# Two engines change the order of two operations inside each step of the second half of the attention

## The chip, the cores and the metric

The kernel runs on one core of a Trainium2 chip. The metric is the time of one execution on the device, in microseconds; below 0.2% (about 4 us here) a change can't be told from none. Five engines matter: PE (TensorE, matrix products), DVE (VectorE), ACT (ScalarE), POOL (GpSimd) and SP, which only issues DMAs. Each engine works off its own list of instructions in order, and they wait for one another on semaphores.

## The reference, cut to what matters

One decoder layer on x of 16 sequences, 128 tokens, 512 columns, in float32:

```
x = x + attention(layernorm(x))          # 16 heads of 128, rms-normed q and k, rope, tanh softcap, causal
x = x + wkv(w, u, layernorm(x), ctx)     # a recurrence over the 128 tokens, channel by channel
x = x + experts(layernorm(x))            # 16 experts, 6 of them per token, and a shared one

# attention, per head:
scores = 50 * tanh(q @ k.T * scale / 50); masked above the diagonal; attn = softmax(scores)
out = attn @ v;  result += out @ wo.T
# wkv, per token t:
no  = max(o, u + k_t);   y = (exp(o - no) p + exp(u + k_t - no) v_t) / (exp(o - no) q + exp(u + k_t - no))
no2 = max(w + o, k_t);   p, q, o = (exp(w + o - no2) p + exp(k_t - no2) v_t,  the same with q and 1,  no2)
```

## The kernel before, in words

Every float32 product is made of three faster ones: each operand is split into a high part (the rounded copy, written by ACT) and a low part (the operand minus its high part, written by DVE or POOL), and PE multiplies high by high, high by low and low by high.

The attention runs in 128 steps and three more that drain it. A step is one pair of heads of one sequence. Its work is spread over four steps by software: in step s PE makes q and k (L976) and v (L1001) of item s (`front`), the scores (L1037) of item s-1 (`mid`), the product of probabilities and v (L1013) and the transposes of its result (L1049) of item s-2 (`back`), and the output product (L1027) of item s-3 (`tail`). PE's order in one step is L976, the transposes of q and k (L166), L1001, L1013, L1027, L1037, L1049. The score part of a step goes: PE scores, ACT tanh (L1245) and exp (L1249) into `ex`, POOL multiplies `ex` by the causal mask (L1422), ACT copies it to the high part of `pT` (L1256), DVE subtracts to get its low part (L1649). L1013 of the next step waits for both parts. DVE then begins the next step with the sums of squares (L1598), the low part of q and k (L1601), which L1037 waits for, and the normalized output (L1616), which L1049 waits for. ACT's part of that is the squares (L1217), for which L1598 waits, and the high part (L1220).

The recurrence needs attention results of finished sequences only. The first half (64 steps) takes the first eight sequences through all eight pairs of heads; the second half takes four sequences at a time. In the second half `rec` is true: one item of the recurrence's own list is worked off in each step (`rec_pe`, `rec_act`, `rec_dve`, `rec_pool`, `rec_pool_norm`, `rec_sp`). A pair of sequences takes a cycle of 11 steps (PITCH), numbered r = 0 to 10 in what follows; two pairs overlap, one in its front part and the one before in its back part. The 64 steps hold the cycles 0 to 4 and nine steps of cycle 5. What the list holds, by r:

| r | DVE (`rec_dve`) | POOL (`rec_pool`, then `rec_pool_norm`) | ACT, at the end of the step |
|---|---|---|---|
| 0 | L482 low part of a row tile; L486 qS*e | L443 pS+vS | L363; L393, which waits for L486 |
| 1 | L490 pS*qS, waits for L447 | L447 pS*e | L373 |
| 2 | L508 scan; L511 | - | - |
| 3 | L498 | L452 | - |
| 4 | L498 | L455 | L401 twice |
| 5 | L494 scan; layer norm statistics (L141 to L148) | L458 | - |
| 6 | - | L462; L152 and L155 | L411, L413 |
| 7 | L518 scan | - | L411, L413 |
| 8 | L518 scan; L523 | - | L419 |
| 9 | L482; L527 | L466 | L423, which waits for L527 |
| 10 | layer norm statistics | L471; L152 and L155, which wait for the statistics | L390 |

Within a step the order on each engine is written out by hand. On DVE the recurrence's item stands after the output's low part (L1637) and ahead of L1649. On POOL it stands after the small operations of the step (L1408, L1411) and the split of a weight piece (L177, which the second half has only in its last four steps) and ahead of the mask (L1422). After the attention come the shared expert's steps (`shared_step`), in which the rest of the recurrence runs, and the routed experts.

Of the kernel before, what the change touches and what calls it, by code (L numbers as in the profile page):

```python
# [56 lines left out]
def build(nc, x, ctxT, weights, qw, kw, cos, sin, wkv_w, wkv_u, gateT, out):  # L57
# [7 lines left out]
    with ExitStack() as ctx:  # L65
# [197 lines left out]
        SPLIT = NSTEP_B // 2  # L263
# [172 lines left out]
        def rec_pool(pool, w):  # L436

            p, r = w // PITCH, w % PITCH
            q, k = p, p - 1
            if r == 0 and 0 <= k < NQ:  # L440
                pool.wait_ge(ev_done, k + 1)
                pool.wait_ge(pm_done, k + 1)
                pool.tensor_tensor(pS[:, :, 0:T], pS[:, :, 0:T], vS[:, :, :], ALU.add).then_inc(num_done, 1)  # L443
            if r == 1 and 0 <= k < NQ:
                pool.wait_ge(num_done, k + 1)
                pool.wait_ge(inv_done, k + 1)
                pool.tensor_tensor(pS[:, :, 0:T], pS[:, :, 0:T], e2[:, :, 1:T + 1], ALU.mult).then_inc(first_done, 1)  # L447
            if not 0 <= p < NQ:
                return
            if r == 3:  # L450
                pool.wait_ge(o_scan, q + 1)
                pool.tensor_tensor(a2[:, :, 1:T + 1], oS[:, :, 0:T], oS[:, :, 1:T + 1],  # L452
                                   ALU.subtract).then_inc(d2_done, 1)
            if r == 4:
                pool.tensor_tensor(e2[:, :, 1:T + 1], kS[:, :, 1:T + 1], oS[:, :, 1:T + 1],  # L455
                                   ALU.subtract).then_inc(e2a_done, 1)
            if r == 5:
                pool.tensor_tensor(dE[:, :, :], kS[:, :, 1:T + 1], oS[:, :, 0:T], ALU.subtract).then_inc(d_done, 1)  # L458
            if r == 6:
                pool.wait_ge(e2_done, q + 1)  # L460
                pool.wait_ge(v_in, 16 * q + 16)
                pool.tensor_tensor(e2v[:, :, 1:T + 1], e2[:, :, 1:T + 1], vS[:, :, :], ALU.mult).then_inc(e2v_done, 1)  # L462
            if r == 9:
                pool.wait_ge(pscan, 2 * q + 2)
                pool.wait_ge(aA_done, q + 1)
                pool.tensor_tensor(pS[:, :, 0:T], pS[:, :, 0:T], aA[:, :, :], ALU.mult).then_inc(pm_done, 1)  # L466
            if r == 10:
                pool.wait_ge(dE_done, q + 1)
                pool.wait_ge(e2v_done, q + 1)
                pool.wait_ge(den_done, q + 1)  # L470
                pool.tensor_tensor(vS[:, :, :], dE[:, :, :], vS[:, :, :], ALU.mult).then_inc(ev_done, 1)  # L471
# [312 lines left out]
        with nc.Block() as block:  # L784
# [588 lines left out]
            def _(pool):  # L1373
# [29 lines left out]
                def step(s, at4, fw, b, g):  # L1403
                    par = at4 % 2
                    front, mid, back, tail, rec = wants(s)
                    if front:
                        pool.wait_ge(ms_done, s + 1)
                        pool.tensor_tensor(rr[:, :], rr[:, :], expo[:, :], ALU.pow).then_inc(pw_done, 1)  # L1408
                        wait(pool, th_done, 2 * s - 2)
                        pool.wait_ge(pw_done, s + 1)  # L1410
                        pool.tensor_tensor(rk[:, par, :], rr[:, HG:4], kscale[:, :], ALU.mult).then_inc(rms_done, 1)  # L1411

                        for n in pieces_of(s):
                            if isinstance(n, int):
                                piece_pool(pool, n, n % 2, (n // HB) % 2, bass.ds(n % HB * PIECE, PIECE))
                            else:
                                piece_pool(pool, n, par, 1 - fw, bass.ds(b * PIECE, PIECE))
                    if rec:
                        rec_pool(pool, s - SPLIT)
                    if mid:  # L1420
                        pool.wait_ge(ex_done, s)
                        pool.tensor_tensor(heads(ex), heads(ex), mask[:, :, :], ALU.mult).then_inc(mask_done, 1)  # L1422
                    if row_tile(s + 1) is not None and s % 2 == 1:
                        ln_pool(pool, row_tile(s + 1) // 2, 0)
                    if rec:
                        rec_pool_norm(pool, s - SPLIT)
                attention(pool, step)
# [90 lines left out]
            def _(dve):  # L1518
# [74 lines left out]
                def step(s, at4, fw, b, g):  # L1593
                    par = at4 % 2
                    front, mid, back, tail, rec = wants(s)
                    if front:
                        dve.wait_ge(sq_done, s + 1)
                        dve.reduce_sum(ssq[:, :], sq.rearrange("p (g n) -> p g n", g=4), AX.X).then_inc(ss_done, 1)  # L1598
                    if mid:
                        dve.wait_ge(qkT_hi, s)  # L1600
                        dve.tensor_tensor(qkT[:, 1, :], QT_[:, :], qkT[:, 0, :].bitcast(F32),  # L1601
                                          ALU.subtract).then_inc(qkT_lo, 1)
                    if front:
                        wait(dve, rms_done, s)
                        dve.wait_ge(ss_done, s + 1)
                        dve.tensor_scalar(rr[:, :], ssq[:, :], 1.0 / DH, RMS_EPS, ALU.mult, ALU.add)\  # L1606
                            .then_inc(ms_done, 1)
                        dve.wait_ge(v_hi, s + 1)
                        dve.tensor_tensor(vE[:, at4, 1, :, 0:DH], heads(V_[:, 0:256]),
                                          vE[:, at4, 0, :, 0:DH].bitcast(F32), ALU.subtract).then_inc(v_lo, 1)  # L1610
                    if back:
                        dve.wait_ge(pv_done, s - 1)
                        av = O_[:, 0:HG * 130].rearrange("p (h n) -> p h n", h=HG)
                        dve.reciprocal(rden[:, :], av[:, :, DH]).then_inc(rden_done, 1)
                        dve.wait_ge(rden_done, s - 1)
                        dve.tensor_tensor(heads(on), av[:, :, 0:DH],  # L1616
                                          rden[:, :].unsqueeze(2).to_broadcast([P, HG, DH]),
                                          ALU.mult).then_inc(on_done, 1)
                    if front:
                        dve.wait_ge(pw_done, s + 1)  # L1620
                        dve.wait_ge(k_out, s + 1)
                        if isinstance(s, int) and s == HB:
                            dve.wait_ge(tabs, 14)
                        for h in range(HG):
                            dve.scalar_tensor_tensor(out=rot[:, h * DH:(h + 1) * DH],
                                                     in0=bank[par][:, h * DH:(h + 1) * DH], scalar=rr[:, h:h + 1],
                                                     in1=rope[:, bass.ds(g * (2 * P) + h * DH, DH)], op0=ALU.mult,
                                                     op1=ALU.mult).then_inc(rot_done, 1)
                    if row_tile(s - 1) is not None:
                        row_lo(row_tile(s - 1), stage[:, row_tile(s - 1) % 2], R_)  # L1630
                    if tail:
                        dve.wait_ge(wo_done, s - 2)
                        bb = behind(s, fw, b, 3)[1]
                        dve.tensor_tensor(xres[:, bb, :], xres[:, bb, :], Y_[:, :], ALU.add).then_inc(acc_done, 1)
                    if back:
                        dve.wait_ge(oT_hi, s - 1)
                        dve.tensor_tensor(oT[:, 1, :, :], heads(OT_[:, 0:256]), oT[:, 0, :, :].bitcast(F32),  # L1637
                                          ALU.subtract).then_inc(oT_lo, 1)
                    if row_tile(s + 1) is not None and s % 2 == 1:
                        n = row_tile(s + 1)  # L1640
                        dve.wait_ge(ld_x, 16 if n < 10 else 32)
                        ln_stats(dve, n // 2, n, 0, used=n)
                    if isinstance(s, int) and 1 <= s <= 12:
                        constants(s)
                    if rec:
                        rec_dve(dve, s - SPLIT)
                    if mid:
                        dve.wait_ge(p_hi, s)
                        dve.tensor_tensor(pT[:, 1, :, :], heads(ex), pT[:, 0, :, :].bitcast(F32),  # L1649
                                          ALU.subtract).then_inc(p_lo, 1)  # L1650

                attention(dve, step)

# [135 lines left out]
```

## Time and profile before

| | |
|---|---|
| time, median of 3 runs | 2057.85 us (2057.79 to 2061.95) |
| the profiled execution, its own time | 2063.05 us |
| its span | 2061.3 us |
| PE busy | 1993.2 us, 97% |
| DVE, ACT, POOL busy | 1073.2, 922.6, 1013.0 us |
| second half of the attention | about 519 to 1045 us of the span |

Busy time is the sum of an engine's instructions. A row of the timeline reads: start, duration, engine, line of the kernel, operation, what it writes <- what it reads, count of instructions merged; in brackets the idle time of the engine just before it and who ended it.

### The profile page before, as it was taken

The numbers are of one execution on the slowest core, as the hardware profiler recorded it, in microseconds if no ns is written. First come the engines' busy times: TensorE is split into PE (matmuls) and PEld (weight loads), VectorE is DVE, ScalarE is ACT, GpSimd is POOL, SyncE is SP. The second block draws the span as 40 slices with busy tenths as digits, with TensorE's granted clock in tenths as the row PEclk, the third lists the DMA queues.
The fourth block names the chain that finished last, engine by engine and source line by source line (L and its number), as shares of the span: only waits on it lengthen the run. The fifth ranks groups of instructions, "written<-read, shape, count | busy, mean of one in ns | idle before, by whom it ended". The sixth has DMA issues, their size and how long they took to land.

```text
span 2061.3 us, 40646 instructions
## 1 busy us (share of the span) xinstructions
PE 1993.2 (97%) x12136; PEld 1804.6 (88%) x12137; DVE 1073.2 (52%) x2351; ACT 922.6 (45%) x2119; POOL 1013.0 (49%) x1076
## 2 busy tenths in 40 slices
PE   6999999999999999999878999899999999999998
PEld 5888888888888888888768899799999999999997
DVE  4765555555667766777666655333333333333332
ACT  4655555554565666657555412233333333233232
POOL 5444444442344444444556206666733333488885
PEclk9999999999999999999989999999999999999999
DMA  9677777777877868777635237666643343499899
GB/s 319 222 235 247 257 249 251 246 245 274 299 257 270 324 238 316 269 264 280 215 95 186 93 102 264 226 205 212 230 137 121 121 127 125 133 214 222 192 215 244
DMA packets 188986, 450.48 MB, mean 219 GB/s; under 512 B 21696, under 2 KB 21952, under 8 KB 188864
## 3 DMA queue, kind: packets, MB, share of 16 engines
q1 hardware_dynamic: 135392, 338.68, 47.8%
q0 software_dynamic: 21504, 51.13, 10.5%
q10 hardware_dynamic: 31968, 59.12, 8.9%
q8 instruction: 67, 1.10, 0.2%
q14 instruction: 55, 0.45, 0.1%
HBM read 275.36 MB, written 173.48 MB: 218 GB/s over the span
## 4 chain that ended last, share of the span: by engine, by line
PE 89%; DMA 3%; POOL 2%; DVE 2%; issue 2%; ACT 1%; SPq 1%; ACTq 0%; POOLq 0%
PE bank L1125 21%; PE bank L976 16%; PE bank L1135 11%; PE bank L1027 8%; PE bank L1001 8%; PE bank L166 6%; PE bank L579 5%; PE bank L1013 4%; PE bank L1037 4%; PE bank L589 3%; PE bank L596 2%; PE bank L1049 1%; DMA xT<-xT_att 1%; DMA raw<-in_weights 1%; POOL w_lo L177 1%
## 5 line engine op out<-in xcount | busy, mean ns | idle before, releaser
L1125 PE MATMUL bank<-w_hi,xT 128*128 x1776 | 473.8, 329 | 2.1 <-DVE xT L1713 2.1
L976 PE MATMUL bank<-w_hi,xT 128*128 128x512 f32 x1024 | 354.3, 407 | 5.0 <-DMA xT<-xT_att 3.5
L1408 POOL TENSOR_TENSOR rr<-rr,expo 128x4 f32<-128x4 f32 x128 | 128.9, 1007 | 423.7 <-DVE rr L1606 423.7
L606 DVE TENSOR_TENSOR hT<-bank,hT 128x384 fp32r<-128x384 f32 x143 | 79.7, 558 | 475.1 <-ACT hT L603 475.1
L1125 PEld LDWEIGHTS bank<-w_hi,xT 128*128 128x128 f32 x1776 | 315.9, 188 | 9.4 <-issue 4.0
L1125 PE MATMUL bank<-w_lo,xT 128*128 x888 | 286.4, 323 | 0.0
L976 PEld LDWEIGHTS bank<-w_hi,xT 128*128 128x128 f32 x1024 | 195.4, 191 | 45.8 <-issue 5.3
L1135 PE MATMUL bank<-w_hi,hT 128*128 x666 | 229.9, 399 | 2.7 <-DVE hT L606 2.5
L603 ACT ACTIVATE hT<-bank 128x384 fp32r<-128x384 f32 x143 | 70.2, 491 | 329.6 <-PE bank L596 315.7
L1001 PE MATMUL bank<-w_hi,xT 128*128 128x256 f32 x1024 | 214.7, 293 | 0.0
L976 PE MATMUL bank<-w_lo,xT 128*128 128x512 f32 x512 | 202.1, 395 | 0.0
L1027 PE MATMUL bank<-w_hi,oT 128*128 128x512 f32 x512 | 189.7, 411 | 0.0
L1245 ACT ACTIVATE th<-bank,rk 128x128 f32<-128x128 f32 x256 | 80.1, 364 | 229.4 <-PE bank L1037 229.4
L1125 PEld LDWEIGHTS bank<-w_lo,xT 128*128 128x128 f32 x888 | 168.1, 189 | 4.2
L1001 PEld LDWEIGHTS bank<-w_hi,xT 128*128 128x128 f32 x1024 | 167.1, 189 | 0.0
L1492 POOL DMA_INDIRECT xres<-yg,a x96 | 148.9, 1551 | 30.3 <-issue 27.4
L1422 POOL TENSOR_TENSOR ex<-ex,mask 128x256 f32<-128x256 f32 x128 | 97.7, 763 | 123.5 <-ACT ex L1249 123.5
L1135 PEld LDWEIGHTS bank<-w_hi,hT 128*128 128x128 f32 x666 | 124.9, 188 | 32.4 <-issue 5.6
L1001 PE MATMUL bank<-w_lo,xT 128*128 128x256 f32 x512 | 144.4, 282 | 0.0
L1598 DVE TENSOR_REDUCE ssq<-sq 128x4 f32<-128x512 f32 x128 | 87.7, 685 | 108.3 <-ACT sq L1217 108.2
L1464 POOL DMA_INDIRECT xg<-xnB,a x96 | 93.8, 977 | 92.0 <-DVE a L708 60.6
L579 PE MATMUL bank<-w_hi,xT 128*128 128x352 f32 x512 | 136.9, 329 | 0.0
(242 smaller groups left out, 4432.6 us busy)
## 6 DMA issues: line engine op xcount, KB each, us to landing
xT<-xT_att SPq DMA_DIRECT2D x126, 512.0 KB, 5.2
w_hi<-w_split SPq DMA_DIRECT2D x64, 512.0 KB, 6.7
w_lo<-w_split SPq DMA_DIRECT2D x64, 512.0 KB, 7.7
xg<-blank SPq DMA_DIRECT2D x111, 264.0 KB, 4.7
yg<-blank SPq DMA_DIRECT2D x111, 256.0 KB, 5.9
raw<-in_weights SPq DMA_DIRECT2D x82, 272.0 KB, 3.1
w_split<-w_hi SPq DMA_DIRECT2D x64, 272.0 KB, 3.4
w_split<-w_lo SPq DMA_DIRECT2D x64, 272.0 KB, 3.7
```

The source lines that it names most:

```text
L166: last = pe.transpose(out[:, c * P:(c + 1) * P], src(c), ident[:, :])
L579: last = pe.matmul(out[:, 0:I], xT[:, par, a, c * P:(c + 1) * P], w_hl[w][:, fw, at:at + I], start=n == 0, stop=n == 11)
L976: last = pe.matmul(bank[par][:, :], xT[:, par, a, c * P:(c + 1) * P], w_hl[w][:, fw, c * 512:(c + 1) * 512], start=n == 0, stop=n == 11)
L1001: last = pe.matmul(V_[:, 0:256], xT[:, par, a, c * P:(c + 1) * P], w_hl[w][:, fw, at:at + 256], start=n == 0, stop=n == 11)
L1027: last = pe.matmul(Y_[:, :], oT[:, a, h, :], w_hl[w][:, bw, at:at + D], start=n == 0, stop=n == 5)
L1125: last = pe.matmul(out_[:, 0:I], xT[:, par, a, c * P:(c + 1) * P], flat(w_hl[w])[:, bass.ds(at + (c * 2 * I + half_ * I), I)], start=n == ...
L1135: last = pe.matmul(out_[:, :], hT[:, a, c * P:(c + 1) * P], flat(w_hl[w])[:, bass.ds(at + (W2_AT + c * D), D)], start=n == 0, stop=n == 3 ...
L1408: pool.tensor_tensor(rr[:, :], rr[:, :], expo[:, :], ALU.pow).then_inc(pw_done, 1)
L1422: pool.tensor_tensor(heads(ex), heads(ex), mask[:, :, :], ALU.mult).then_inc(mask_done, 1)
L1464: pool.indirect_dma_start(out=xg[:, :], out_offset=bass.IndirectOffsetOnAxis(ap=slot_i[:, k, b:b + 1], axis=0), in_=xnB[:, b, :], in_offse ...
L1492: pool.indirect_dma_start(out=xres[:, b, :], out_offset=None, in_=yg[:, :], in_offset=bass.IndirectOffsetOnAxis(ap=slot_i[:, k, b:b + 1], ...
L1598: dve.reduce_sum(ssq[:, :], sq.rearrange("p (g n) -> p g n", g=4), AX.X).then_inc(ss_done, 1)
```

## The change

In the steps of the attention (`step` of POOL and of DVE) two blocks swap places. POOL applies the mask (L1422) ahead of `rec_pool`; `rec_pool_norm` stays last. DVE makes the low part of the probabilities (L1649) ahead of `rec_dve`. No instruction is added or removed, and no wait changes. In the first half, where `rec` is false, the order is the same as before.

```diff
@@ POOL, step @@
-                    if rec:
-                        rec_pool(pool, s - SPLIT)
                     if mid:
                         pool.wait_ge(ex_done, s)
                         pool.tensor_tensor(heads(ex), heads(ex), mask[:, :, :], ALU.mult).then_inc(mask_done, 1)
                     if row_tile(s + 1) is not None and s % 2 == 1:
                         ln_pool(pool, row_tile(s + 1) // 2, 0)
+                    if rec:
+                        rec_pool(pool, s - SPLIT)
                     if rec:
                         rec_pool_norm(pool, s - SPLIT)
@@ DVE, step @@
-                    if rec:
-                        rec_dve(dve, s - SPLIT)
                     if mid:
                         dve.wait_ge(p_hi, s)
                         dve.tensor_tensor(pT[:, 1, :, :], heads(ex), pT[:, 0, :, :].bitcast(F32),
                                           ALU.subtract).then_inc(p_lo, 1)
+                    if rec:
+                        rec_dve(dve, s - SPLIT)
```

## Rows read from the trace of the kernel before

**Rows 1.** The page, busy time by engine:
```profile
PE 1993.2 (97%) x12136; PEld 1804.6 (88%) x12137; DVE 1073.2 (52%) x2351; ACT 922.6 (45%) x2119; POOL 1013.0 (49%) x1076
```

**Rows 2.** Waits of PE, 585 to 1060 us: total us, times, longest:
```profile
PE bank L1013 <- issue: 10.7, 6, 3.3
```

**Rows 3.** Timeline, 827 to 838 us, a step with r = 5 and the next:
```profile
827.51 2.40 POOL L458 TENSOR_TENSOR dE<-kS,oS 128x1024 f32<-128x1024 f32 x1
...
829.32 0.42 ACT L1249 ACTIVATE ex<-th 128x256 f32<-128x256 f32 x1
...
829.87 0.74 POOL L1422 TENSOR_TENSOR ex<-ex,mask 128x256 f32<-128x256 f32 x1
...
830.38 2.38 DVE L494 TENSOR_TENSOR_SCAN qS<-a,e 128x1032 f32<-128x1032 f32 x1
...
834.35 0.42 DVE L1649 TENSOR_TENSOR pT<-ex,pT 128x256 fp32r<-128x256 f32 x1
834.68 0.68 DVE L1598 TENSOR_REDUCE ssq<-sq 128x4 f32<-128x512 f32 x1
834.87 0.86 PE L1013 MATMUL bank<-vE,pT 128*128 128x130 f32 x6 [1.37 <-issue]
...
837.63 0.41 PE L1049 MATMUL bank<-ident,on 128*128 128x128 f32 x2
```

**Rows 4.** DVE against POOL: timeline at 1068 and 519 us; lines (duration ns min/median/max):
```profile
1068.73 2.21 POOL L443 TENSOR_TENSOR pS<-pS,vS 128x1024 f32<-128x1024 f32 x1
...
1068.87 3.14 DVE L486 TENSOR_TENSOR qS<-qS,e 128x1024 f32<-128x1024 f32 x1
...
518.90 0.42 DVE L1649 TENSOR_TENSOR pT<-ex,pT 128x256 fp32r<-128x256 f32 x1
...
519.07 0.80 POOL L152 TENSOR_TENSOR rstd<-rstd,expo 128x2 f32<-128x2 f32 x1 [1.67 <-DVE rstd L148]
...
L486 DVE TENSOR_TENSOR qS<-qS,e x8: 1215/1440/3143, 609.6 to 1158.0; 128x1024 f32<-128x1024 f32 x8
...
L152 POOL TENSOR_TENSOR rstd<-rstd,expo x24: 692/722/1469, 6.4 to 1179.3; 128x2 f32<-128x2 f32 x24
```

**Rows 5.** Timeline, 860 to 869 us, a step with r = 9 and the next:
```profile
860.42 2.19 POOL L466 TENSOR_TENSOR pS<-pS,aA 128x1024 f32<-128x1024 f32 x1
...
861.55 0.42 ACT L1249 ACTIVATE ex<-th 128x256 f32<-128x256 f32 x1
...
862.61 0.68 DVE L482 TENSOR_TENSOR stage<-bank,stage 128x512 fp32r<-128x512 f32 x1
863.21 1.22 DVE L527 TENSOR_TENSOR qS<-qS,dE 128x1024 f32<-128x1024 f32 x1
...
866.65 0.69 DVE L1598 TENSOR_REDUCE ssq<-sq 128x4 f32<-128x512 f32 x1 [1.89 <-ACT sq L1217]
...
868.93 0.44 PE L1049 MATMUL bank<-ident,on 128*128 128x128 f32 x2
```

**Rows 6.** Timeline, 869 to 874 us, the step with r = 10:
```profile
869.39 2.41 POOL L471 TENSOR_TENSOR vS<-dE,vS 128x1024 f32<-128x1024 f32 x1
...
870.58 0.42 ACT L1249 ACTIVATE ex<-th 128x256 f32<-128x256 f32 x1
...
873.53 0.42 DVE L1649 TENSOR_TENSOR pT<-ex,pT 128x256 fp32r<-128x256 f32 x1
...
873.96 0.69 DVE L1598 TENSOR_REDUCE ssq<-sq 128x4 f32<-128x512 f32 x1
```

**Rows 7.** Timeline, 877 to 883 us, the step with r = 0:
```profile
877.67 0.42 ACT L1249 ACTIVATE ex<-th 128x256 f32<-128x256 f32 x1
...
879.33 1.34 DVE L486 TENSOR_TENSOR qS<-qS,e 128x1024 f32<-128x1024 f32 x1
...
882.28 0.69 DVE L1598 TENSOR_REDUCE ssq<-sq 128x4 f32<-128x512 f32 x1 [1.28 <-ACT sq L1217]
```

**Rows 8.** Busy us of each engine (xcount), PEclk granted, DMA share, GB/s, 1018 to 1025 us:
```profile
1018.00:1025.00 7.00, 6.41 (x22) 5.71 (x23) 3.88 (x12) 3.97 (x11) 5.03 (x5) 0.51 0.21 52
```

## The prediction

> **What bounds the kernel now.** I read the page first: PE is busy 97% of the span [rows 1], so almost every microsecond that PE stands still is a microsecond of the kernel, and time can be won or lost only there. The view of waits for PE, cut to the second half of the attention, then shows what there is to win: 10.7 us in six waits of L1013, the longest 3.3 [rows 2]. The releaser is not named ("issue"), but the timeline names it [rows 3]: in a step with r = 5, DVE goes from the scan L494 at 830.38 through the layer norm statistics to L1649 at 834.35, and L1013, which needs its result, starts at 834.87 after an idle of 1.37. So 3.97 us of recurrence stand ahead of a 0.42 us operation that PE needs. The other thing to see there is who paces PE when DVE is late: L1049 needs L1616, a fixed distance behind L1598. In rows 5, L1049 starts 2.28 after L1598 (866.65 to 868.93), and that is the shortest distance there can be; in rows 3 it is 2.95 (834.68 to 837.63), so there L1049 had 0.67 us in hand. The question for each step is therefore when L1598 starts.
>
> **The change, part by part.** POOL's mask now starts as soon as the exp is done: 0.05 after it, and it takes 0.74 (L1422 in rows 3). In rows 3 it started 0.13 after the exp's end (829.74 to 829.87) because L458 ended only then, so this gain is 0.1 us; elsewhere up to 0.8 us. The probabilities' low part no longer waits for the recurrence, so the six waits of rows 2 should go. That is the plus side, and for PE it is worth nothing by itself if the same recurrence work then delays L1598.
>
> What is late next is just that. Two things are added ahead of L1598. First, L1649 must wait for mask and copy before DVE's recurrence may begin, where DVE used that time. Second, and larger, POOL's recurrence operation used to run beside DVE operations that read PSUM; now it starts when the mask ends, about 0.5 us before L1649 is ready to start (the 0.42 us copy lies between), and lies across L1649 and what follows it. Rows 4 show what happens when two such operations meet: L486, which reads two SBUF tensors and takes 1.22 at its shortest, started 0.14 after POOL's L443 and took 3.14. L443 ended at 1070.94 and L486 at 1072.01, 1.07 later: it stood still until L443 was through, with 0.15 of its start-up hidden. L1649 is of the same kind (`ex` and `pT` are both in SBUF), and in the other direction it is seen to hold POOL up: POOL's L152, 0.69 at its shortest, took 0.80 beside it and ended 0.55 after L1649's end (519.32 to 519.87). No row shows L1649 itself behind a long POOL operation. Its cost there is between 0 and the whole POOL operation less the 0.5 us head start, 1.4 to 1.9 us; I take the upper end, since L486 is the nearest row: L1649 ends 0.27 (0.42 less 0.15) after POOL's recurrence operation.
>
> The Trainium skill, page "SBUF — State Buffer", section "Who interferes with whom", says that a VectorE instruction with two SBUF inputs contends with a GpSimd instruction that reads SBUF and that the one issued first blocks the other fully; by it the upper end holds for L1649 too. The page "Advanced Engine Details and Errata", section "Mode Summary", names only VectorE's two-port modes as interfering, and a float32 tensor_tensor is not one; by that alone neither L1649 nor L486 would wait, and the sum would be the third rival's below. The 3.14 us of L486 [rows 4] speaks for the first.
>
> Now each costly step, as exp's end + 0.05 + mask 0.74 - 0.04 (POOL operations overlap by that) + POOL's operation + 0.27 = L1649's end, then DVE's recurrence (each starting 0.07 before the last ends), then L1598:
> - r = 5 [rows 3]: exp ends 829.74, L458 takes 2.40, L1649 ends 833.16. The scan and the statistics take 3.97, so L1598 starts at 837.06 instead of 834.68. L1049 follows at +2.28, 839.34 instead of 837.63: **+1.7 us**. The wait of L1013 is gone, and a longer one of L1037 and L1049 stands in its place. Without any blocking L1649 would end at 831.4, L1598 start at 835.3 and L1049 at 837.6: nothing won or lost.
> - r = 9 [rows 5]: exp ends 861.97, L466 takes 2.19, L1649 ends 865.18. L482 takes 0.60 to L527, and L527 1.22: it ends at 866.93. L423 on ACT waits for L527, and ACT's squares come after it. One such ACT operation and the squares put 1.61 between DVE's end and L1598 (L486 ends 880.67, L1598 starts 882.28, rows 7). So L1598 starts at 868.54 instead of 866.65: **+1.9**, and L1049 with it.
> - r = 10 [rows 6]: exp ends 871.00, L471 takes 2.41, L1649 ends 874.43. The statistics are 3.97 less the scan's 2.31, 1.66: L1598 at 876.02 instead of 873.96, **+2.1**.
> - r = 0 [rows 7]: exp ends 878.09, L443 takes 2.21 [rows 4], L1649 ends 881.32. L482 and L486 (0.60 + 1.22) end at 883.07, and L1598 starts 1.61 later, 884.68 instead of 882.28, +2.4. PE is ahead of DVE in this stretch, so the exp can come up to 0.9 us earlier against the L1598 before it (estimate); I take **+1.6**.
> - The other steps: r = 1 and 3 to 8 have 0.7 to 2.4 us of recurrence on DVE, and by the same sum L1598 starts up to 1.4 us late in them. L1049's slack in a step is about as much (estimate; 0.67 was left even in rows 3, in which PE had waited 1.37): nothing, at most 0.3 each.
>
> r = 9, 10 and 0 follow one another with PE waiting for DVE, so their delays add: 5.6 us. The second half holds five such groups, the first with little in it (no L482, no back part): 4 x 5.6 + 3 = 25.4 us. It holds six steps with r = 5: four like rows 3, 4 x 1.7 = 6.8; the first, without statistics and without a wait before, +1.7; the last, which has the 3.3 us wait of rows 2 in it and weight pieces on POOL, +0.5 (it may as well gain 2). Sum: 34.4 us.
>
> **The clock.** After the 3.3 us wait the granted clock was 0.51 over the next 7 us [rows 8], half of 2.4 GHz; at half speed that cost about 3.4 us. After the waits of 1.37 it stayed full. The new waits with r = 5 are about 3 us long, close to the one that lost the clock, and PE must work at full pace behind them. Between 0 and 4 x 3.4 = 14 us: I take 5.
>
> Against the profiled execution, 2063.05 us, the sum gives 2063.05 + 34.4 + 5 = 2102.5. That execution was 5.2 us above the median of 2057.85, so for the median I forecast 2097 us.
>
> **The rivals.**
> - L1649 isn't blocked, only the long DVE operations are (L527, L486). Then r = 5 costs nothing, r = 9 about 1 us and r = 0 about 0.6, 8 to 10 us in all: 2067 us. For it: no row shows L1649 blocked. Against: it reads two SBUF tensors as L486 does, and holds up L152.
> - Faster: L1013's waits go and L1049's slack takes up the rest. That is 4 x 1.6 and the 3.3 us wait with its clock loss, 3.3 + 3.4: 13 us, 2045 us. It decides by whether L1598 of the step after r = 5 starts by about 833.7 (L1049 would fall due at 837.63 - 1.6 = 836.0, less 2.28). Against: the scan and statistics alone end at 834.7 even if they start right behind a free L1649 at 830.8.
> - No blocking of any kind, as the second page has it: only the time DVE loses before its recurrence counts, 0.5 to 0.6 us for r = 9, 10 and 0 in each group, 5 x 1.5 = 7 us: 2065 us.
> - The clock falls after nearly every wait of 2 us and more: 14 us and more instead of 5, 2110 to 2120 us.
>
> **How the numbers follow.** Forecast 70%, its own range 2084 to 2110; first and third rival together 14%; faster 7%; the clock 9%. I give 2066 to 2114, which holds the forecast, the two mild cases' upper part and half of the last. Under 0.2% (4 us) a difference can't be told: faster 0.07, same 0.03, slower 0.90.
>
> **What the changed profile would show.** L1649 with a median near 2 us in steps with POOL work, against 0.42 now: the central step, and if it stays at 0.42 the first rival holds. No waits of L1013 in the second half, and in their place waits of L1049 for L1616 and of L1037 for L1601. L1598 later than now by the four numbers above, counted from the step's exp. A PEclk below 9 between 600 and 1000 us for the clock term. Wrong would be a second half no longer than now, or L1013 still waiting.

## The result, and the profile after

The change makes the kernel slower. Measured together: 2103.99 us (median of 4 runs, 2098.17 to 2107.05) against 2058.82 us before (2057.79 to 2061.95), a ratio of 1.021, 95% interval 1.0194 to 1.0225 (the ratios in this document are estimated over all runs of a series and differ a little from the quotient of the two medians). The forecast was 2097 in a range of 2066 to 2114, with 0.90 for slower. The profiled execution took 2107.05 us (forecast for it: 2102.5), its span 2105.3.

The page after, busy time by engine (answers to [rows 1]), the same page's row of the probabilities' low part (now L1647; the mask is now L1420), and its PEclk row, in tenths:

```profile
PE 2013.5 (96%) x12136; PEld 1815.2 (86%) x12137; DVE 1135.6 (54%) x2351; ACT 926.0 (44%) x2119; POOL 1012.8 (48%) x1076
...
PEclk8999999999999999999998999999999999999999
...
L1647 DVE TENSOR_TENSOR pT<-ex,pT 128x256 fp32r<-128x256 f32 x128 | 122.2, 955 | 71.2 <-ACT pT L1256 71.1
```

The same instructions on every engine; DVE is busy 62.4 us longer. The 64 low parts of the second half took 26.6 us together before and 95.1 after, 68.5 more: that is more than all of it, and some of DVE's other operations got shorter (the scan L494: median 2.41 before, 2.29 after).

The waits of PE in the second half (total us, times, longest), answering to [rows 2]:

```profile
PE bank L1037 <- ACT qkT L1220: 17.8, 10, 2.0
PE bank L1037 <- issue: 15.7, 9, 2.8
PE bank L1013 <- issue: 3.4, 5, 1.4
PE bank L976 <- DMA xT<-xT_att: 0.9, 2, 0.7
PE bank L1013 <- ACT pT L1256: 0.8, 1, 0.8
```

The waits of L1013 fell from 10.7 to 3.4 us, and 33.5 us of L1037 stand where 0.9 us stood before. That is the whole trade in five lines: PE waits little for the probabilities now; it waits for the next item's q and k instead.

The timeline after, the step with r = 5 that answers to [rows 3]:

```profile
854.97 0.42 ACT L1249 ACTIVATE ex<-th 128x256 f32<-128x256 f32 x1
855.46 0.74 POOL L1420 TENSOR_TENSOR ex<-ex,mask 128x256 f32<-128x256 f32 x1 [0.92 <-ACT ex L1249]
856.16 2.42 POOL L458 TENSOR_TENSOR dE<-kS,oS 128x1024 f32<-128x1024 f32 x1
856.24 0.42 ACT L1256 ACTIVATE pT<-ex 128x256 fp32r<-128x256 f32 x1 [0.58 <-POOL ex L1420]
856.69 2.17 DVE L1647 TENSOR_TENSOR pT<-ex,pT 128x256 fp32r<-128x256 f32 x1 [0.57 <-ACT pT L1256]
858.78 2.29 DVE L494 TENSOR_TENSOR_SCAN qS<-a,e 128x1032 f32<-128x1032 f32 x1
...
858.98 0.83 PE L1013 MATMUL bank<-vE,pT 128*128 128x130 f32 x6
...
862.65 0.68 DVE L1598 TENSOR_REDUCE ssq<-sq 128x4 f32<-128x512 f32 x1
...
864.03 1.51 PE L1037 MATMUL bank<-qkT 128*128 128x128 f32 x6 [2.76 <-issue]
```

L458 runs from 856.16 to 858.58. L1647 starts 0.53 behind it and ends at 858.86, 0.28 after it, though alone it takes 0.42. L1598 starts 7.26 after the exp's end. L1037 then takes 1.51 instead of 0.86: the granted clock has fallen to half of 2.4 GHz, as the window behind it shows (PEclk is the third number from the end; answers to [rows 8]):

```profile
863.30:870.10 6.80, 6.07 (x19) 5.14 (x20) 5.11 (x11) 2.64 (x7) 4.58 (x5) 0.50 0.90 364
```

The same in the steps with r = 9 and 10 (answering to [rows 5] and [rows 6]):

```profile
892.66 2.20 POOL L466 TENSOR_TENSOR pS<-pS,aA 128x1024 f32<-128x1024 f32 x1
...
893.19 1.96 DVE L1647 TENSOR_TENSOR pT<-ex,pT 128x256 fp32r<-128x256 f32 x1 [0.58 <-ACT pT L1256]
...
898.49 0.69 DVE L1598 TENSOR_REDUCE ssq<-sq 128x4 f32<-128x512 f32 x1 [1.61 <-ACT sq L1217]
...
903.60 2.39 POOL L471 TENSOR_TENSOR vS<-dE,vS 128x1024 f32<-128x1024 f32 x1
...
904.12 2.14 DVE L1647 TENSOR_TENSOR pT<-ex,pT 128x256 fp32r<-128x256 f32 x1 [0.57 <-ACT pT L1256]
...
907.86 0.68 DVE L1598 TENSOR_REDUCE ssq<-sq 128x4 f32<-128x512 f32 x1
```

**Where the 44 us went, step by step.** PE paces the attention, so the gap between the L1049 of successive steps is the length of a step; the gap at r runs from the L1049 of that step to that of the next. The table has the gap after minus the gap before, taken from the two timelines, for each r and each of the cycles 0 to 5. The rows left out hold 0.1 or less, except one 0.94 at r = 2 (a wait of L976 for its DMA) and -2.4 at r = 8 of cycle 5, the last gap, which lies behind the stretch measured next (there the kernel before has a wait of L1013 of 1.95 us and a fall of the clock).

```
r     cycle 0     1     2     3     4     5     sum
9          1.33  1.92  1.42  1.92  1.92         8.5
10         1.69  1.73  1.83  1.49  1.71         8.4
0          0     0.76  1.99  2.34  2.23  1.99   9.3
1          0     0.05  0.84  1.61  1.89  1.52   5.9
4          0.07  0.07  0.05  0.05  0.06 -2.21  -1.9
5          1.56  1.94  1.66  2.07  1.98 -1.02   8.2
6          0.02  1.06  0.02  2.21  1.03  0.98   5.3
```

With the 0.94 at r = 2, and without the last gap, it is 44.6 us; the second half, from L1598 of its first step to that of its last, went from 516.6 to 560.7 us. What follows it took 1023.9 us after and 1025.4 before. So the loss lies in the steps that the prediction named, and in the steps with r = 1 and 6 right behind them, to which it gave no wait.

The -2.21 at r = 4 of cycle 5 is a wait for a DMA in the profiled execution of the kernel before; nothing in the runs ties it to the change.

```profile
1002.90 0.47 PE L976 MATMUL bank<-w_hi,xT 128*128 128x512 f32 x1 [2.02 <-DMA xT<-xT_att]
```

Waits of L976 of this kind come at other places in other executions (1.43 us at about 997 in the second run of the one-mask kernel below, 1.76 at about 650 in the second run with filler), so differences of about 2 us between the second halves of two profiles can be chance. The changed kernel's second half was 560.7 us in this profile and 557.7 in another.

Below, "second half" is that span. It is also what is compared between chips: on one of them (the runs against 2126.35 us below) the kernel before was some 65 us slower. In the kernels profiled there the extra lies behind the second half (1085.1 us in the one-mask kernel, against 1025.7 on the other chip). Times are compared only with the kernel before on the same chip.

### The profile page after: what moved, and what is told of

Its sections match the earlier page's. It is cut to its first block, busy times and chain, and to the rows that moved or that the text cites. A ratio compares the mean times of both kernels' runs of the same rounds, so it can differ in the third digit from the quotient of the medians.

```text
span 2105.3 us, 40646 instructions
## 1 busy us (share of the span) xinstructions
PE 2013.5 (96%) x12136; PEld 1815.2 (86%) x12137; DVE 1135.6 (54%) x2351; ACT 926.0 (44%) x2119; POOL 1012.8 (48%) x1076
## 4 chain that ended last, share of the span: by engine, by line
PE 82%; DVE 5%; issue 4%; POOL 3%; DMA 3%; ACT 2%; SPq 1%; ACTq 0%; POOLq 0%
PE bank L1125 20%; PE bank L976 14%; PE bank L1135 11%; PE bank L1027 7%; PE bank L1001 7%; PE bank L166 5%; PE bank L579 4%; PE bank L1037 3%; PE bank L1013 3%; PE bank L589 3%; PE bank L596 2%; DMA xT<-xT_att 1%; PE bank L1049 1%; DVE pT L1647 1%; POOL rr L1408 1%
## 5 line engine op out<-in xcount | busy, mean ns | idle before, releaser
L976 PE MATMUL bank<-w_hi,xT 128*128 128x512 f32 x1024 | 365.6, 419 | 3.5 <-DMA xT<-xT_att 2.4
L1125 PEld LDWEIGHTS bank<-w_hi,xT 128*128 128x128 f32 x1776 | 315.8, 188 | 9.3 <-issue 3.9
L976 PEld LDWEIGHTS bank<-w_hi,xT 128*128 128x128 f32 x1024 | 202.7, 198 | 47.0 <-DMA xT<-xT_att 2.8
L976 PE MATMUL bank<-w_lo,xT 128*128 128x512 f32 x512 | 208.1, 406 | 0.0
L1420 POOL TENSOR_TENSOR ex<-ex,mask 128x256 f32<-128x256 f32 x128 | 94.8, 740 | 171.7 <-ACT ex L1249 171.7
L1001 PEld LDWEIGHTS bank<-w_hi,xT 128*128 128x128 f32 x1024 | 167.4, 190 | 0.1
L1647 DVE TENSOR_TENSOR pT<-ex,pT 128x256 fp32r<-128x256 f32 x128 | 122.2, 955 | 71.2 <-ACT pT L1256 71.1
L1037 PEld LDWEIGHTS bank<-qkT 128*128 128x128 f32 x768 | 105.0, 193 | 52.9 <-ACT qkT L1220 21.9
```

What stands on the lines that cost most here:

```text
L976: last = pe.matmul(bank[par][:, :], xT[:, par, a, c * P:(c + 1) * P], w_hl[w][:, fw, c * 512:(c + 1) * 512], start=n == 0, stop=n == 11)
L1001: last = pe.matmul(V_[:, 0:256], xT[:, par, a, c * P:(c + 1) * P], w_hl[w][:, fw, at:at + 256], start=n == 0, stop=n == 11)
L1037: last = pe.matmul(S_[:, h * T:(h + 1) * T], qkT[:, a, (HG + h) * T:(HG + h + 1) * T], qkT[:, w, h * T:(h + 1) * T], start=n == 0, stop=n ...
L1125: last = pe.matmul(out_[:, 0:I], xT[:, par, a, c * P:(c + 1) * P], flat(w_hl[w])[:, bass.ds(at + (c * 2 * I + half_ * I), I)], start=n == ...
```

## The experiments

**DVE's half alone.** DVE in the new order, POOL in the old one.

```diff
@@ DVE, step; POOL as before @@
-                    if rec:
-                        rec_dve(dve, s - SPLIT)
                     if mid:
                         dve.wait_ge(p_hi, s)
...
+                    if rec:
+                        rec_dve(dve, s - SPLIT)
```

> DVE's half of the change alone: the low part of the probabilities ahead of the recurrence on DVE, POOL's order as before. Theory A (a DVE operation with two SBUF inputs and a POOL operation exclude each other; in the changed kernel POOL's recurrence operation lies on L1649 and the DVE recurrence): here POOL's operation is over before the mask, so the low-part operation keeps its 0.42 us, but it has to wait for mask and copy, which POOL's operation delays by up to 0.8 us, and DVE's recurrence waits behind it. From the timeline of before: r = 5 about 0, r = 9 +0.9, r = 10 +1.1, r = 0 +1.6 us, in 4.5 groups 16 us, so 2070 to 2078 us; few or no falls of the clock before 1000 us. Rival B (no blocking; what costs in the changed kernel is that POOL's results arrive 2 to 3 us later and the recurrence's chain becomes late): POOL's order is untouched, so at most +7 us, 2058 to 2065 us.

Measured: 2082.9 us against 2060.31, ratio 1.0102 (1.0085 to 1.0119), above the 2070 to 2078 expected. The low part takes 0.42 to 0.43 us in each step, and still half of the loss is there. The waits of PE and the step with r = 5:

```profile
PE bank L1037 <- ACT qkT L1220: 15.6, 10, 1.9
PE bank L1037 <- issue: 9.3, 11, 2.8
...
839.91 2.40 POOL L458 TENSOR_TENSOR dE<-kS,oS 128x1024 f32<-128x1024 f32 x1
...
843.48 0.43 DVE L1647 TENSOR_TENSOR pT<-ex,pT 128x256 fp32r<-128x256 f32 x1 [0.61 <-ACT pT L1256]
843.82 2.30 DVE L494 TENSOR_TENSOR_SCAN qS<-a,e 128x1032 f32<-128x1032 f32 x1
```

So moving DVE's recurrence behind the low part has a price of its own. By the table's measure it is 1.0 to 1.6 (r = 9), 0.5 to 0.8 (10), 1.9 to 2.3 (0, from the third cycle on), and nothing at r = 5 but in the last cycle. The expectation had 0.9 for r = 9, and few or no falls of the clock before 1000 us: there are three, behind the waits of r = 0, at 1.6 us each.

**POOL's half alone.** POOL in the new order, DVE in the old one (the diff's POOL part).

> POOL's half alone: the mask ahead of POOL's recurrence operation, DVE's order as before. Theory A: POOL's operation now lies on DVE's own recurrence operations. L527 and L486 should take 2 to 3 us instead of 1.2 to 1.5, L494 either its 2.4 (if it gets hold first) or 4.5, the low part 0.42 in most steps and up to 1 us with r = 10. Sum per cycle 2.9 to 4.6 us, 13 to 21 us in all: 2070 to 2080 us. Rival B: POOL's results are as late as in the changed kernel, so most of its +45 us should be here, over 2085 us, while the durations of DVE's operations stay as before.

Measured: 2089.33 us, 1.0127 (1.0109 to 1.0145). The time is in the range that was to speak against the theory (over 2085 us), but the durations of DVE's operations, which were to stay as before in that case, show blocking, and the cost is more than the expectation had counted:

```profile
846.18 2.34 DVE L494 TENSOR_TENSOR_SCAN qS<-a,e 128x1032 f32<-128x1032 f32 x1
846.31 4.36 POOL L458 TENSOR_TENSOR dE<-kS,oS 128x1024 f32<-128x1024 f32 x1
...
850.68 0.41 DVE L1649 TENSOR_TENSOR pT<-ex,pT 128x256 fp32r<-128x256 f32 x1
...
851.20 1.29 PE L1013 MATMUL bank<-vE,pT 128*128 128x130 f32 x6 [1.91 <-issue]
...
858.11 1.96 DVE L1649 TENSOR_TENSOR pT<-ex,pT 128x256 fp32r<-128x256 f32 x1 [0.57 <-ACT pT L1256]
```

Here DVE's scan began 0.13 before POOL's L458 and kept its 2.34; L458 took 4.36 instead of 2.40 and ended 2.15 after the scan. So each engine can hold up the other: in these rows and in those of the changed kernel the operation that started first kept its time, and the other stood until it was over. That is called the lock in what follows. With DVE in the old order L1649 is blocked too where DVE has nothing or little to do before it (1.96 in the row at 858.11, r = 6). L1013 waits 21.7 us in all, twice the figure before. Neither half of the change gains.

**Whose cost is the blocked low part?** The changed kernel, with POOL holding its recurrence back until the low part is made.

```diff
+                        pool.wait_ge(p_lo, s)
                         rec_pool(pool, s - SPLIT)
```

> The changed kernel with one wait more: POOL begins its recurrence operation only when the low part of the step's probabilities is done. POOL's results arrive later still, but L1649 (L1647 in it) has no POOL operation beside it. Theory A: its duration falls from a median of about 2 us in steps with POOL work to 0.42; r = 5 gets back 1.7 us and r = 10 about 1.3 (r = 9 and r = 0 nothing, since L527 and L486 are then blocked in its place), 15 us in all, and some of the falls of the clock go: 2080 to 2090 us, that is faster than the changed kernel's 2104 although a wait was added. Rival B: every result of POOL is later, so it is slower than the changed kernel, over 2106 us.

Measured: 2098.16 us, 1.0173 (1.0155 to 1.0191), between the two theories' ranges. The low part fell to 0.42 in every step, as foretold. In the first five steps with r = 5 and in those with r = 10 together, 10.4 us came back. At r = 9 and 0 nothing did from the second group on, because POOL's operation now meets what is next on DVE:

```profile
901.59 0.42 DVE L1648 TENSOR_TENSOR pT<-ex,pT 128x256 fp32r<-128x256 f32 x1 [0.56 <-ACT pT L1256]
...
902.09 2.39 POOL L471 TENSOR_TENSOR vS<-dE,vS 128x1024 f32<-128x1024 f32 x1 [0.99 <-DVE pT L1648]
...
903.13 0.30 DVE L144 BATCH_NORM_AGGREGATE mv<-st 128x2 f32<-128x6 f32 x2
...
903.46 1.05 DVE L147 TENSOR_SCALAR nmean<-mv 128x2 f32<-128x2 f32 x1
904.43 0.15 DVE L148 TENSOR_SCALAR rstd<-mv 128x2 f32<-128x2 f32 x1
...
910.26 2.20 POOL L443 TENSOR_TENSOR pS<-pS,vS 128x1024 f32<-128x1024 f32 x1 [0.99 <-DVE pT L1648]
...
910.70 2.85 DVE L486 TENSOR_TENSOR qS<-qS,e 128x1024 f32<-128x1024 f32 x1
```

L486 took 2.85 instead of 1.21 and ended 1.09 after L443. And L147, an operation on two columns that takes 0.17 alone, stood until L471 was through (904.48), while the statistics ahead of it (L141, L144) passed freely. By the table: r = 5 costs 0.5 instead of 1.6 and r = 10 0.8 to 1.0 instead of 1.7, but r = 9 and 0 cost 1.5 to 2.3 and 2.1 to 2.5. That the collision moves there instead of ending, the expectation had said. What it had not is that r = 1 and 6 lose 9 us more than in the changed kernel: the clock falls eleven times, and 6.3 us are one step (r = 1, cycle 1) in which L976 waited 3.21 us for its DMA, with a fall of 6.8 us behind it. Why that load came late is not shown.

**Is the lock held for a whole instruction?** The changed kernel, each of POOL's eight recurrence operations cut in two halves of 128x512.

```diff
+            for h in (slice(0, KC), slice(KC, 2 * KC)):
+                pool.tensor_tensor(out[:, h, :], a[:, h, :], b[:, h, :], op).then_inc(done, 1)
```

(and the waits for these semaphores count twice as far)

> The changed kernel with each of POOL's eight recurrence operations (128x1024) in two halves (128x512), every result the same. Theory A, that L1649 (L1647 here) stands still until the POOL instruction that began before it is over: the first half takes about 1.2 us (0.74 for 256 elements and 2.2 for 1024 give 0.26 + 0.48 per 256), L1647 is ready 0.5 after its start and ends 0.27 after its end, so its duration in steps with POOL work falls from 1.96 to 2.16 us to about 1.0. The second half then lies on DVE's recurrence instead, so the time changes little, 2095 to 2105 us. Rival: the two engines share bandwidth while they overlap; then L1647 overlaps POOL's work as long as before and its duration stays at about 2 us.

Measured: 2161.73 us against 2126.35, 1.018 (1.0125 to 1.0236); second half 550.8 us, 9.9 and 6.9 below the changed kernel's two profiles. The step with r = 5:

```profile
852.88 2.73 POOL L438 TENSOR_TENSOR dE<-kS,oS 128x512 f32<-128x512 f32 x2
853.41 1.04 DVE L1649 TENSOR_TENSOR pT<-ex,pT 128x256 fp32r<-128x256 f32 x1 [0.57 <-ACT pT L1258]
854.37 3.40 DVE L496 TENSOR_TENSOR_SCAN qS<-a,e 128x1032 f32<-128x1032 f32 x1
```

The low part fell from 2.17 to 1.04: it got through between the halves. Then the second half met the scan, which took 3.40 instead of 2.29. So the lock is held for one instruction at a time; two engines that share bandwidth for as long as they overlap would have left the low part as it was.

**What must leave the step with r = 5?** The kernel before, with the variance and mean of the row tile (the statistics, 1.66 us of DVE) taken one step later, from r = 5 to r = 6, in which DVE has nothing else. Order of both engines as before.

```diff
-            if r == 5 and back:
+            if r == 6 and back:
```

> The kernel before with one edit: the layer norm statistics of the recurrence (1.66 us on DVE) move from r = 5 to r = 6, where DVE has nothing. By the timeline of before, L1649 of r = 5 then ends 8.3 us after L1598 and L1013 falls due at 8.6: the four waits of 1.4 us (1.6 us in the spacing of the matmuls) go, and the last, of 3.3 us, shrinks by 0.5 only, because there the mask is held up by L494. L1598 of the next step comes 1.7 earlier too, so nothing takes their place. 4 x 1.6 + 0.5 = 7 us: 2050 to 2053 us. The rival: the statistics delay ACT's norm in r = 7 or L1598 after r = 6 by as much, 2057 to 2060 us.

Measured: 2052.67 us against 2060.31, 0.9966 (0.9949 to 0.9983); on another chip, in the run below, 0.9955. Faster than both kernels. In that second run the second half takes 507.4 us, 9.2 less than before. The table's measure is -1.6 in each of four steps with r = 5. In the last cycle it is -2.6 at r = 5, with 1.5 lost again at r = 6, and -2.1 at r = 4, which is the DMA wait of 2.02 us that the kernel before had there; so some 7 us are the edit's. What the change wanted, L1013 not waiting for the probabilities, comes in these four steps from less work in the full step, not from another order.

**The same in the changed kernel.**

> The changed kernel with the layer norm statistics moved from r = 5 to r = 6 on DVE, as in the run e5. By the sum of the prediction L1598 after r = 5 comes 1.66 us earlier, so the waits of L1037 there shrink by as much, 5 x 1.7 = 8 us, and the falls of the clock behind them (four or five of the ten in the second half) go, up to 6 us more: 2088 to 2098 us. It stays 35 us or more above the same edit without the change (2052.7), since r = 9, 10 and 0 are as in the changed kernel. Rival: with the list of DVE at r = 5 short, putting the low part first costs nothing any more, and it comes to within 10 us of 2052.7.

Measured: 2154.26 against 2126.35, 1.0116 (1.0062 to 1.0171); second half 546.0, 14.7 and 11.7 us below the changed kernel's two profiles and 38.6 above the last one. Steps with r = 5 and 6 together cost 0.6 instead of 1.6; r = 9, 10 and 0 cost the same 1.9, 1.7 and 2.0 to 2.3. The three steps are independent of the statistics, as the sum had them.

**The mask early in one step alone.** The kernel with later statistics, in which L1013 still waited 2.7 us behind the last step with r = 5; POOL's mask ahead of its recurrence there and nowhere else.

```diff
-                    if rec:
+                    if rec and s != NSTEP_B - 4:
                         rec_pool(pool, s - SPLIT)
                     if mid:
...
+                    if rec and s == NSTEP_B - 4:
+                        rec_pool(pool, s - SPLIT)
```

> The run e5 (statistics at r = 6, otherwise the kernel before) with POOL's half of the change in one step only, the first of the last four steps (r = 5 of the last cycle), where POOL also splits two weight pieces and the mask began at 7.7 and took 2.7 us because L494 had got ahead of it. With the mask before POOL's recurrence operation it starts at 5.4, L494 gets ahead of POOL's operation instead (as the run e2 showed, where L494 took 2.34 and L458 4.37), and L1649 ends at 8.7 us against 8.6 at which L1013 falls due. The wait of 2.9 us there and the fall of the clock behind it (3.4 us) go: 5 us less than e5, 2046 to 2050 us. Rival: POOL's operation, which then ends at about 10.7, delays L1408 of the next step and through it the transposes of L166, and the gain is gone: 2052 us.

Measured: 2113.79 us against 2126.35, 0.9948 (0.9922 to 0.9974); second half 506.5 us, 0.8 below that of the kernel with later statistics alone (507.3 in its first run), not 5. The step, from the second run of it; the last row is the same L1013 without the early mask, from the second run of that kernel:

```profile
1006.30 2.64 DVE L494 TENSOR_TENSOR_SCAN qS<-a,e 128x1032 f32<-128x1032 f32 x1
1006.73 4.36 POOL L458 TENSOR_TENSOR dE<-kS,oS 128x1024 f32<-128x1024 f32 x1
...
1008.86 2.52 DVE L1651 TENSOR_TENSOR pT<-ex,pT 128x256 fp32r<-128x256 f32 x1
...
1011.48 0.86 PE L1013 MATMUL bank<-vE,pT 128*128 128x130 f32 x6 [2.06 <-issue]
...
1011.59 0.86 PE L1013 MATMUL bank<-vE,pT 128*128 128x130 f32 x6 [2.69 <-ACT pT L1256]
```

A chain of locks: the scan holds up L458, and L458, once it has the lock, holds up the low part until it ends at 1011.09. L1013 waits 2.06 instead of 2.69. Even the one early mask takes only 0.6 us off a wait of 2.7, since the long operation put behind it holds up the low part in turn.

**The clock.** The changed kernel, with products that nothing reads ahead of the waits for the low part of q and k, 282 of them in the steps with r = 6, 10 and 1, some 36 us of PE's time laid into the waits. They write the bank of the scores, which L1037 then overwrites, so the wait for its last reader (`th_done`) moves ahead of them.

```diff
+                        wait(pe, th_done, 2 * s - 2)
+                        if rec and s > SPLIT + 5:
+                            old = vE[:, (at4 - 2) % 4, 0, :, :].rearrange("p h n -> p (h n)")
+                            for n in range({6: 22, 10: 14, 1: 16}.get((s - SPLIT) % PITCH, 0)):
+                                pe.matmul(S_[:, 0:256], old[:, 0:P], old[:, 0:256], start=True, stop=True)
                         pe.wait_ge(qkT_hi, s)
                         pe.wait_ge(qkT_lo, s)
-                        wait(pe, th_done, 2 * s - 2)
```

> The changed kernel with filler products on PE, ahead of its waits of L1037, in the steps with r = 6 (22 products of 256 columns, 2.6 us), r = 1 (16, 1.9 us) and r = 10 (14, 1.7 us) from the second cycle on; they write into the scores' bank, which L1037 overwrites, and fit into the waits of 2.9, 2.1 and 2.0 us there. They add work and take no wait away. Theory: the falls of the granted clock (ten in the second half against one before) come from PE's idle time in those waits and cost time, 13 us by the spacing of the matmuls in the stretches at half speed. Then there are three falls or fewer, and the time is 2091 to 2097 us, less than the changed kernel's 2104, with more work done. Rival: the falls cost nothing, since DVE sets the pace there, or don't hang on the idle time: 2104 us or more.

Measured: second half 551.9 us with no fall of the clock in it, against 560.7 with ten in the changed kernel's first profile; the whole time, 2173.31 us against 2126.35 (1.0139 to 1.0255), left the question open. So four kernels ran once more on one chip, the kernel before at 2062.34 us there. The changed kernel:

> The changed kernel as it is, so that the three kernels beside it are compared with it on one chip. Both theories: 1.018 to 1.022 of before, second half about 560 us with about ten falls of the granted clock, of which about 16 us of TensorE's time are lost.

2103.97 us, 1.0197 (1.018 to 1.0214). With filler:

> The changed kernel with products that nothing reads ahead of the waits for the low part in r=6, 10 and 1. In its first run the falls of the clock in the second half went from ten to none and the half got 8.8 us shorter. If the clock is a cost of its own behind the waits: 8 to 12 us below the changed kernel on this chip, that is a ratio of about 1.015 to before. If the falls only coincide with waits and cost nothing: equal to the changed kernel or above it, as the added products have to be run.

2098.68 us, 1.0171 (1.0154 to 1.0188): 5.3 us less for 36 us more of work, where 8 to 12 us had been expected. The intervals meet, so the traces must carry it: no fall in the second half (555.1 us) against ten (557.7). Four windows of 100 us (busy us of each engine, PEclk, DMA share, GB/s), first of the changed kernel in this series:

```profile
600.00:700.00 100.00, 92.45 (x566) 80.55 (x565) 76.86 (x150) 58.93 (x132) 40.80 (x46) 0.97 0.72 258
700.00:800.00 100.00, 94.83 (x568) 82.92 (x567) 74.31 (x144) 54.74 (x125) 40.38 (x45) 0.93 0.69 244
800.00:900.00 100.00, 92.11 (x579) 80.95 (x580) 78.09 (x155) 59.06 (x132) 41.86 (x47) 0.98 0.73 258
900.00:1000.00 100.00, 92.34 (x563) 80.90 (x562) 74.87 (x145) 54.83 (x127) 39.82 (x44) 0.95 0.69 241
```

and of the one with filler:

```profile
600.00:700.00 100.00, 95.73 (x615) 84.72 (x615) 75.14 (x145) 57.06 (x128) 40.63 (x45) 1.00 0.72 254
700.00:800.00 100.00, 97.55 (x635) 86.70 (x635) 77.31 (x151) 57.81 (x132) 40.81 (x46) 1.00 0.71 254
800.00:900.00 100.00, 98.42 (x637) 87.44 (x637) 77.29 (x152) 58.79 (x133) 41.73 (x48) 1.00 0.73 254
900.00:1000.00 100.00, 98.42 (x641) 87.48 (x639) 77.72 (x148) 58.19 (x133) 43.50 (x47) 1.00 0.74 260
```

By the table's measure, the kernel with filler loses what the changed one does at r = 9, 10 and 0 (8.5, 8.4, 9.5 us; the changed kernel of the same series 8.6, 8.3, 9.3) and 1.61 to 1.64 in each step with r = 5 from the second cycle to the fifth. But at r = 1 it loses only 0.6, where the changed kernel lost 2.5 in the same series and 5.9 in the first profile, and at r = 6 1.1 instead of 7.0 and 5.3. So nearly all of these two rows is the clock: PE at half of 2.4 GHz behind a wait, 9.5 us in the one profile and 11.2 in the other, of which 1.7 are left. The filler gives much of it back: 3.3 us in two longer stretches in which L976 waited for its DMA (4.2 us of such waits, where the view of the changed kernel in that series lists none), 1.1 us in the first r = 5. And of the 1.1 left at r = 6, 1.0 is the last cycle, where a wait of L1013 of 1.30 us stands in the place of the fall.

**The two faster kernels side by side.**

> Before, with the recurrence's variance and mean moved from r=5 to r=6. On one chip it was at 0.9966 of before, 7.6 us. The same here: 6 to 10 us below before, second half 506 to 509 us.

2054.03 us, 0.9955 (0.9939 to 0.9972).

> The last kernel with GpSimd's mask first in one step alone. In its first run its second half was only 0.8 us shorter than that of the last kernel. If the blocked low part gives back what the early mask gains: within 2 us of the last kernel on this chip. If its first time, 0.9948 of before, was the mask's gain: 3 to 5 us below it.

2054.01 us, 0.9959 (0.9945 to 0.9973), second half 508.1 us against 507.4: no difference. The early mask's 0.9948 on the other chip was not its gain.

## Why the prediction was right, and where a term was off

- **The step that carried the forecast holds.** L1647 took 1.95 to 2.18 us in the steps with r = 0, 4, 5, 6, 9 and 10, in which POOL has a tensor_tensor of the recurrence, 1.65 and 1.76 in r = 3 and 1, whose POOL operation is shorter, and 0.42 in r = 2, 7 and 8, which have none. Wherever it was blocked it ended 0.27 to 0.29 after POOL's operation. Halving POOL's operations halved it, holding them back removed it. The first and third rival are out: their mild cases asked for 2065 to 2067 us. The Trainium skill, page "SBUF — State Buffer", section "Who interferes with whom", has this blocking as a rule for a VectorE instruction with two SBUF inputs, and the trace agrees for the low part too, 2.17 against 0.42.
- **The four places of L1598.** Counted from the exp's end, forecast and measured (cycle 3 as in the rows shown, and r = 0 of cycle 4): r = 5: 7.32 and 7.26; r = 9: 6.57 and 6.60; r = 10: 5.02 and 5.03; r = 0: 6.59 and 6.60.
- **What they cost PE.** r = 5: 1.7 forecast, 1.6 measured; r = 9: 1.9 and 1.3 to 1.9; r = 10: 2.1 and 1.5 to 1.8; r = 0: 1.6 and 2.0 to 2.3. The group of three: 5.6 forecast, 5.59 to 5.64 measured in four groups, 3.8 in the first (forecast 3). The other steps: nothing to 0.07 (forecast up to 0.3).
- **The sum.** Groups 26.3 us (forecast 25.4), the first five r = 5 at 1.6 each 8.1 (8.5). The last r = 5 is -1.0 in the table, but the kernel before lost 2.4 us of clock in that gap (from L1013 to L1049 it took 5.15 us, against 2.76 in rows 3); without the clock it is +1.4 (forecast +0.5). Together 35.8 against 34.4.
- **The mis-sized term is the clock.** Forecast 5 us in bounds of 0 to 14, "the new waits with r = 5 are about 3 us long". Measured: 5.9 at r = 1, 5.3 at r = 6 and 1.1 at r = 5 (what its five steps have above 1.63), less the 2.4 of before: 9.9 us; by the same sum 7.8 in the second profile of the changed kernel, again with ten falls. Two things were wrong in it. The granted clock fell ten times, where 5 us stand for one or two falls at 3.4: after four of the r = 5 waits, and also behind the waits of r = 9, 10 and 0, which are 0.6 to 2.0 us each and follow one another (four falls in r = 1, two in r = 10). And a fall of 3.4 us length cost 0.8 to 1.9 us; the forecast's 3.4 was for a stretch of 7 us, and the one such stretch after, 863.3 to 870.1, cost 2.7; the two in r = 10 cost nothing (1.69 and 1.49 there; with filler and no fall 1.71 and 1.49), because PE would have waited for DVE anyway. Too few falls and too high a price for one partly cancelled: that is luck. The fourth rival, a fall after nearly every wait of 2 us, named the mechanism better than the forecast did; with its price per fall it came out at 2110 to 2120 and so too high.
- **35.8 + 9.9 + 0.9 (r = 2) - 2.2 (the DMA wait of before at r = 4) + 0.3** is 44.7 on 2063.05: 2107.7, for 2107.05 measured. The terms are read from the same two profiles, so this shows that none is missing and proves nothing more. The DMA wait, which brings the measured sum nearer to the forecast, is luck as well.
- **What the halves add.** The forecast called blocking the larger of its two causes. Each half alone costs 22.6 and 29.0 us, the whole 42 to 45: neither order has a cause to itself. With DVE's half alone the low part isn't blocked, but the mask stands behind POOL's operation; with both, the low part is blocked by the operation. Either way it ends after POOL's operation, and the recurrence on DVE comes after that. So the forecast's ranking of the two isn't borne out.
- **Not as foretold:** "no waits of L1013 in the second half" was too much: 3.4 us are left, 1.4 of them behind the last r = 5, and 0.5 to 0.6 in each of three steps after r = 10, in which L1647 is held until POOL's L471 ends. And the waits foretold for L1049 are not in the view of waits: all stand at L1037, which comes before it on PE. The distance from L1598 to L1049, 2.28, held in the steps after r = 9, 10 and 0 (2.27 to 2.28). One reading in the forecast is off without harm: the rival of a faster kernel has a free L1649 end at 830.8, where the forecast's own sum for r = 5 has 831.4, and the later end speaks against that rival still more.

## What to carry to other kernels

When VectorE has operations with two SBUF inputs and GpSimd works on SBUF beside it, putting the urgent small operation first on both engines can start GpSimd's long one right in front of VectorE's, as it did here: before choosing the order, work out where each long operation will lie and what it will overlap. A wait removed by a new order in a step with full engines came back at the next deadline; moving work into a step with room gave 0.3 to 0.4% with one changed number. Waits of 1.7 to 2.0 us had falls of TensorE's clock behind them as waits of 2.8 us did; whether it takes several in a row is not shown (the kernel before has a fall behind a single one of 1.95). So price the wait and the slow stretch behind it apart.

## What the runs showed that had not been expected

- A tensor_scalar with one SBUF input, 128x2 float32, is blocked as well: L147 took 1.05 us instead of 0.17, until POOL's operation ended (the kernel before has it too, up to 1.01). The same page and section of the Trainium skill says that tensor_scalar can enter modes that take the shared port, when its operands meet their conditions, and the row fits that; the statistics' own instructions (L141, L144) were not held up.
- The scan (tensor_tensor_scan, two SBUF inputs) takes part in the lock both ways: it lengthened L458 from 2.40 to 4.36, and took 3.40 instead of 2.29 behind half an operation of POOL.
- Useless products in the waits took the falls of the clock in the second half from ten to none, and the 9.5 us lost at r = 1 and 6 in the same series to 1.7, at the price of 36 us of extra work in PE's idle time. The kernel's median was 5.3 us lower for it, with intervals that meet.
